# Second attention: two PSUM banks for turned probabilities and two for projections, in place of one and three

## The reference

```
scale = sqrt(256)
Q = einsum('bqd,hdk->hbqk', q, w_qs)
K = einsum('bsd,hdk->hbsk', k, w_ks)
V = einsum('bsd,hdv->hbsv', v, w_vs)
scores = einsum('hbqk,hbsk->hbqs', Q, K) / scale
attn = softmax(where(mask, -inf, scores), axis=-1)
out = einsum('hbqs,hbsv->hbqv', attn, V)
lin = concat_heads(out) @ W_o.T + b_o
z = lin + q
result = (z - mean(z)) / (std(z, ddof=1) + 0.001) * gamma + beta
```

## Time and profile before

| | |
|---|---|
| median of 3 runs | 1602.48 us (1601.96 to 1604.83) |
| the profiled execution, its own time | 1601.42 us |
| its span (first to last instruction) | 1599.6 us |
| busy: PE, PEld, DVE, ACT, POOL | 83%, 66%, 54%, 51%, 27% |
| second attention, prelude and pairs | about 716 to 1400 us of the span |
| granted PE clock, mean of the span | 0.924 of full speed |

### The profile page before, as it was taken

The page is one execution under the profiler, slowest core; times in us unless marked ns, Lnnn a source line. Parts: engine busy times, 40 slices in busy tenths (PEclk is TensorE's granted clock), DMA queues, the critical chain, the costliest instruction groups (busy, mean ns, idle before and its releaser), DMA issues. The chain is left out here.

```text
span 1599.6 us, 36282 instructions
## 1 busy us (share of the span) xinstructions
PE 1329.8 (83%) x10688; PEld 1048.8 (66%) x10689; DVE 870.9 (54%) x2881; ACT 809.8 (51%) x2219; POOL 434.1 (27%) x810
## 2 busy tenths in 40 slices
PE   5598898889549999539999999999999999539992
PEld 3466666666438888538778787878777877326661
DVE  4375666656434645356566666767676767212223
ACT  3476776666434544355555555645454555113332
POOL 5234544444322231210011212121212121312221
PEclk8799999999769999859999999999999999569996
DMA  7562322220033531220000000000000013311114
GB/s 226 198 224 74 104 94 71 97 90 25 12 116 132 182 128 59 85 98 22 11 12 12 21 11 21 11 21 10 21 10 21 0 38 159 116 30 59 59 59 136
DMA packets 45589, 114.97 MB, mean 72 GB/s; under 512 B 8876, under 2 KB 29036, under 8 KB 41808
## 3 DMA queue, kind: packets, MB, share of 16 engines
q1 hardware_dynamic: 37444, 95.62, 17.8%
q0 software_dynamic: 7168, 14.99, 2.9%
q10 hardware_dynamic: 880, 3.28, 0.6%
HBM read 70.42 MB, written 47.65 MB: 74 GB/s over the span
## 5 line engine op out<-in xcount | busy, mean ns | idle before, releaser
L774 ACT ACTIVATE b_prob<-b_prob,b_low 100x361 f32<-100x361 f32 x256 | 154.9, 605 | 99.9 <-DVE b_low L886 99.9
L623 PE MATMUL b_ps_p<-b_context_part,b_wk_part 128*128 128x362 f32 x768 | 158.6, 344 | 0.0
L782 ACT COPY b_prob_t<-b_ps_t 128x300 f32<-128x300 f32 x256 | 103.3, 404 | 106.6 <-PE b_ps_t L687 103.4
L1470 ACT ACTIVATE a_prob<-a_prob,a_low 100x361 f32<-100x361 f32 x256 | 153.2, 601 | 0.1
L1478 ACT COPY a_prob_t<-a_ps_t 128x300 f32<-128x300 f32 x256 | 97.4, 406 | 109.2 <-PE a_ps_t L1373 91.3
L629 PE MATMUL b_ps_p<-b_wv_part,b_context_part 128*128 128x512 f32 (+1 forms) x576 | 151.5, 405 | 0.0
L886 DVE CUSTOM_DVE_ANT_0 b_prob<-b_ps_s,b_mask_bias 100x361 f32<-100x361 f32 x256 | 121.4, 530 | 37.3 <-PE b_ps_s L677 22.2
L687 PE MATMUL b_ps_t<-ident,b_prob 100*128 100x100 f32 x768 | 119.1, 265 | 24.2 <-ACT b_prob_t L782 23.9
L1613 DVE CUSTOM_DVE_ANT_0 a_prob<-a_ps_s,a_mask_bias 100x361 f32<-100x361 f32 x256 | 121.4, 531 | 32.4 <-PE a_ps_s L1363 25.0
L623 PEld LDWEIGHTS b_ps_p<-b_context_part,b_wk_part 128*128 128x128 f32 x768 | 125.4, 190 | 0.2 <-issue 0.2
L1373 PE MATMUL a_ps_t<-ident,a_prob 100*128 100x100 f32 x768 | 105.5, 262 | 24.0 <-ACT a_prob_t L1478 22.3
(11 more groups left out here) (301 smaller groups left out, 2668.2 us busy)
## 6 DMA issues: line engine op xcount, KB each, us to landing
rows_in<-zero SPq DMA_DIRECT2D x44, 514.0 KB, 5.8
w<-in_c_fc SPq DMA_DIRECT2D x8, 1024.0 KB, 8.4
w<-in_c_proj SPq DMA_DIRECT2D x8, 1024.0 KB, 5.0
a_context<-in_ctx SPq DMA_DIRECT2D x16, 361.0 KB, 3.5
b_context<-in_ctx SPq DMA_DIRECT2D x16, 361.0 KB
rows_in<-rows_in SPq DMA_DIRECT2D x8, 514.0 KB, 5.0
f_xe<-rows_in SPq DMA_DIRECT2D x8, 514.0 KB
f_xe<-rows_in SPq DMA_DIRECT2D x32, 128.5 KB, 2.1
```

The costliest lines, as they stand in the source:

```text
L623: ins = nc.tensor.matmul(bank[:, 0:LN2], w_parts["k"][a][:, k, t * P:(t + 1) * P], cx_parts[s][b][:, k, :], start=m == 0, stop=m == DK * l ...
L774: nc.scalar.activation(prob[0:S, k, 0:L], prob[0:S, k, 0:L], ACT.Exp, bias=low[0:S, k:k + 1], scale=-1.0, accum_out=total[0:S, k:k + 1]).t ...
L1470: nc.scalar.activation(prob[0:S, k, 0:L], prob[0:S, k, 0:L], ACT.Exp, bias=low[0:S, k:k + 1], scale=-1.0, accum_out=total[0:S, r:r + 1]).t ...
```

## The change

Turned probabilities get two banks, used in turn, and turn k waits for the copy of turn k-2. The projections get two banks in place of three: unit u waits until unit u-2 is taken. The units, their order, their shapes and every other engine's program stay as they are (the count of 42 units divides by two as by three, with the same one empty unit).

```
-BANKS = 3
+BANKS = 2
...
-    ps_t = ps("ps_t")
+    ps_t = [ps(f"ps_t{k}") for k in range(2)]
...
-                pe.wait_ge(pt_ready.sem, pt_ready.at(j, k))
+                pe.wait_ge(pt_ready.sem, pt_ready.at(j, k - 1))
                 for c in range(KT_N):
-                    ins = nc.tensor.transpose(ps_t[:, c * S:(c + 1) * S], prob[0:S, k % PAIR_PB, c * P:(c + 1) * P],
+                    ins = nc.tensor.transpose(ps_t[k % 2][:, c * S:(c + 1) * S], prob[0:S, k % PAIR_PB, c * P:(c + 1) * P],
                                               T["ident"][0:S, 0:S])
                 ins.then_inc(turned.sem, 1)
...
-                nc.scalar.copy(pt[:, k % PAIR_PT, :], ps_t[:, 0:KT_N * S]).then_inc(pt_ready.sem, 1)
+                nc.scalar.copy(pt[:, k % PAIR_PT, :], ps_t[k % 2][:, 0:KT_N * S]).then_inc(pt_ready.sem, 1)
```

## The result

The changed kernel takes **1667.94 us** (median of 4 runs, 1665.42 to 1668.47) against 1602.22 us for the kernel before on the same chip (4 runs, 1601.63 to 1604.83): a ratio of 1.0404, 95% interval 1.0386 to 1.0422, or 65.7 us more. The forecast was 1657, some 55 more, with a range of 1636 to 1676.

The account below looks back on a forecast made before the run. PE was taken to bound the second attention. Six pairs at 7.4 gave 44.4, first pair 6, last pair 0, tail -2, prelude 3, clock 3: +54.4 us on 1601.42, stated as 1657, range 1636 to 1676.

Parts of the forecast that it names:

- step 4: Second attention, step 4 of a pair: units 16 and 18 wait for banks, 2.03 and 1.12, together 3.15 us lost.
- steps 1 to 3 and 5 to 7: Bank waits in a pair: 1.3 us lost over steps 1 to 3; 1.81, 1.68 and 1.55 in steps 5, 6, 7.
- the restart: PE resumes 0.14 us behind the end of what it waits for, read at a turn and used for every wait.
- What the second turned bank gives: Step 0 of a pair: turn 1 and the second K run without the turned-bank wait, a gain of 1.31 us.
- the clock: One or two more falls of PE's granted clock, at about 1.9 us each: +3 us in all.
- Rival 3: Waits in steps 4, 5 and 7 lower the clock; ten more falls than counted, 1677 us and up; chance 0.08.
- First pair: The first pair, without turns in step 0 or real W, N, G and C of a pair before: +6 us.
- Up to the first score: The prelude: K units slowed by two banks, 1.4 us, and as much for the query units: +3 us.
- Behind the seventh pair: The last pair's later steps have turns and nearly no units, so turn waits go: -2 us.
- Rival 1: ACT and DVE free projection banks in time, so only turn waits go and the kernel gets faster, 1579 us; chance 0.02.
- Rival 2: Takers gain while PE waits, leaving one short wait a step: 2 to 4.5 us a pair, 1617 to 1635; chance 0.09.
- Rival 4: Scaling L899 ends last, so steps 0, 5 and 7 keep their turn waits; about 1657 to 1668 us; chance 0.02.

Follow-up runs that it names:

- the kernel with the added matmuls: The changed kernel with six unused matmuls into a free turned bank ahead of the empty unit's wait in step 0; 1662.02 us, ratio 1.0370.
- the repetition: The changed kernel, unaltered, measured and profiled once more; 1667.12 us, ratio 1.0408.
- The kernel with copies first on the changed one: The changed kernel with ACT's copies of turns 0 and 1 of a step ahead of the exponents; 1690.26 us, ratio 1.0541.

## Why the prediction was right or wrong

**Right: the direction and its mechanism.** The turn waits went from 23.9 to 3.6 (forecast: under 9), though six of the eight left stand in step 7, at 0.44, and not in step 0. The waits for DVE L824 and L750 came, 43.9 us in all, just under the forecast 45 to 65. The first wait of unit 16 is the longest of them and is released by DVE L750: 1.79 of idle, where the sum had 2.03. With one turned bank as before and two projection banks the time is the same, which shows that the banks of the projections are the cost. Only the shortest full pair, at 89.8 us, is within the forecast 88 to 90; the other five take 91.0 to 95.7.

**Right in size: step 4.** Steps without a stretch at the lower level, after less before: step 4 loses 3.04, forecast 3.15.

**Too large: steps 1 to 3 and 5 to 7, and the restart.** Steps 1 to 3 lose 0.95 together (0.25 + 0.31 + 0.39), forecast 1.3. For step 1 the one full pair must be taken that isn't behind a fall, 9.08 against 8.83; the kernel with the added matmuls, which has no fall there, shows 9.05 to 9.08 in all six. Steps 5 to 7 lose 0.91, 1.26 and 1.26, where the sum had 1.81, 1.68 and 1.55. Part of this is the restart. The 0.14 was read from a turn behind ACT's copy and used for every wait. It holds there, and the unit that waits for DVE's copy L750 starts 0.13 behind it; but the K, V, Q and router units that wait for a subtraction start 0.05 to 0.06 behind it, in every such wait of the changed kernel's trace (the W unit of step 2: 0.13). Nine terms of a pair rest on such waits, which makes 0.8 too much. The other 0.5 or so beyond the 0.8 taken off fits takers that come earlier, and was not tested. Over six pairs, steps 1 to 7 without falls lose 7.42 x 6 = 44.5, where the sum has (9.5 - 0.8) x 6 = 52.2.

**Wrong: step 0.** The sum had a gain of 1.31 a pair there. Measured is a loss: the six steps 0 take 52.2 us in place of 45.4. That is +6.7 against -7.9, 14.6 us, the largest miss of the sum, with the clock falls of step 0 in it. The step that failed is "What the second turned bank gives". It followed the turns and the second K, which came out nearly as worked out, and then stopped, and it held that only units that project ask for a bank. The empty unit asks too, at unit 2, where the taking two units back is the first of its pair. This is shown by the run in which it doesn't ask: step 0 falls to 6.05, 1.38 under the 7.43 of before. But even then the gain doesn't last. Step 1 takes 10.08 there against 9.08 in the changed kernel, because its second score group waits for DVE's copy of the outputs (7.6 us in all). That leaves about 0.4 of the 1.31: the sum ended at turn 2 and did not ask what PE meets next.

The clock's share of the 6.7 can be estimated from the kernel with the added matmuls, which has no fall in step 0: its six steps 0 take 47.1. The fall in step 0 of the kernel before cost 1.9, so without falls the loss is about 47.1 - 43.5 = 3.6, and the miss of this term 11.5.

**Too small: the clock.** The sum had one or two more falls, +3. The profile has ten stretches against two, the repetition twelve. The six full pairs went from 493.0 to 552.9, 59.9 more; with the estimate above, the falls cost 59.9 - 44.5 - 3.6 = 11.8 of it net, four times the term. Rival 3 was this mechanism with ten more falls than counted at 1.9 each; there were about seven more, at 1.2 to 1.6 each where they can be read. The falls stand behind waits of 1.8 to 2.5 us in steps 0 and 4 and at a wait of 1.28 in step 7. In step 0 every wait that long has one, in the other two not: all six full pairs have the waits of steps 4 and 7, two have a fall in step 4 and three in step 7. What decides that stays open.

**The rest.** First pair +5.7 (forecast 6). Up to the first score +5.0 (forecast 3): the K units of the prelude take 1.38 more, forecast 1.4, and what is left is mostly the query units, of which six in place of five stand behind their first bank wait, at a clock that rises later (0.89 over the 26.0 us up to the first score, against 1.00 over 20.6). Behind the seventh pair -6.6 (forecast -2): one part is the turn waits, 5.6 us by the run with one turned bank; that stretch's clock is also 0.88 in place of 0.86.

The misses together (step 0, steps 1 to 7, clock, up to the first score, first pair, behind the seventh): 11.5 - 7.7 + 8.8 + 2.0 - 0.3 - 4.6 = 9.7, against 64.0 - 54.4 = 9.6. The range held in part by luck: two losses that were missed and one that was counted too high stood against each other.

**The rivals.** Rival 1 (takers keep up) would need PE's list without the new waits; they are there. The rule of the Trainium skill named beside it (Perfetto Trace Analysis, Optimization Strategy), that a gap repeating on the engine to be saturated may call for more PSUM, was right as to where the gap was; the bank that it asks for brought nothing here when it came out of the projections' rotation: with two projection banks the pairs took 630.8 us without it and 631.0 with it. With three it could not be tried. Rival 2 (PE's queue gives most back) is true in part in steps 5 to 7. Rival 4 fell with the 3.6 us.

**Not tried.** Three projection banks with two turned ones, for which the kernel has no bank left. POOL's L542 moved away from the scaling L899; the pairs in which the two don't meet suggest that it is 0.5 to 0.7 us of the waits of 2.34 and 2.45 at the empty unit.

## What to carry to other kernels

A bank that no wait in the profile names is not spare: set the start of each unit beside the end of the taking two units back before a rotation is shortened, and include the slots that do nothing, for they wait too. Read the restart from a wait on the same engine: it was 0.14 us behind ACT's copy and 0.05 behind DVE's subtraction. And follow a gain until the next thing that PE may have to wait for. A visible wait for a buffer can be the order of work on the engine that empties it; trying that order first costs no buffer, and here it gave what the bank didn't (0.9926 alone, 0.9821 with the next wait in the chain ended as well). The same reordering was worth -11 us with three banks and +23 with two: an edit's price holds only for the slack beside it.

## What was unexpected of the hardware

The scaling L899 on DVE, 100 x 361 in f32, took 1.41 us while POOL's tensor-tensor L542 ran, and 0.39 right behind it. The kernel with copies first on the changed one shows the same pair of durations:

```profile
1019.20 1.59 POOL L542 TENSOR_TENSOR b_context_part<-b_context,b_context_part 128x722 fp32r<-128x722 f32 x1 [0.19 <-DVE b_low L888]
...
1019.76 1.23 DVE L901 TENSOR_SCALAR b_prob<-b_prob,b_inv 100x361 f32<-100x361 f32 x1
...
1021.42 0.39 DVE L901 TENSOR_SCALAR b_prob<-b_prob,b_inv 100x361 f32<-100x361 f32 x1
```

It ends 0.20 us behind POOL's end in both. The twelve traces of this case hold 83 scalings that start while L542 runs. They last 0.49 to 1.80 us, and every one ends 0.20 to 0.21 behind the end of L542, wherever it started; those that no L542 overlaps have a median of 0.40. So the scaling is held until POOL is done, in every case on record; why is not shown, and no run took the one away from the other. The masked score L886, which reads PSUM, keeps its 0.53 when it starts beside L542.

And the clock: PE's waits of 1.3 to 2.5 us, some of them followed by a stretch at 1.2 GHz, so that such a wait can cost 1.2 to 1.6 more behind it than its own length. Adding 36 matmuls that nobody reads went with a stage 7 us shorter in the profiled execution.
